# A chain of two attention and two Mamba layers on one core: softplus gathered in one visit, norm shifts moved from GpSimd to VectorE, C rows later in their queue, and a new order

## What is computed

```python
xz = einsum('bsd,ed->bse', xn, in_proj_w);  x_in, z = split(xz, 2)
u = silu(conv1d(x_in) + conv_b)                    # 512 channels, 4 taps
dt_r, B, C = split(einsum('bsd,ed->bse', u, x_proj_w), [64, 80])
dt = softplus(einsum('bsr,dr->bsd', dt_r, dt_proj_w) + dt_proj_b)
A = -exp(A_log)                                    # 16 states per channel
def step(h, inp):
    dt_t, B_t, C_t, u_t = inp
    h = h * exp(dt_t[:, :, None] * A) + (dt_t * u_t)[:, :, None] * B_t[:, None, :]
    return h, einsum('bdn,bn->bd', h, C_t)
y = (scan(step) + u * D_param) * silu(z)
out = x + gate * einsum('bsd,ed->bse', y, out_proj_w)
```

## Time and profile before

| | us |
|---|---|
| median of 3 runs | 2023.14 |
| lowest of 3 runs | 2008.57 |
| the profiled execution | 2021.5 |
| its span, first to last instruction | 2019.3 |

### The profile page before, as it was taken

One profiled execution on the slowest core, in us unless ns is written; L12 is line 12 of the kernel. 1 busy time (PEld: TensorE's weight loads), 2 busy tenths in 40 slices (PEclk: granted clock), 3 DMA queues, 4 the chain that ended last, 5 costly groups with the idle time before them and its releaser, 6 DMA issues. The chain is left out here.

```text
span 2019.3 us, 29111 instructions
## 1 busy us (share of the span) xinstructions
PE 1817.7 (90%) x9252; PEld 1265.7 (63%) x9252; DVE 1780.9 (88%) x1818; ACT 1710.2 (85%) x3224; POOL 1789.5 (89%) x823
## 2 busy tenths in 40 slices
PE   8979688998989999998999999898998999697778
PEld 7555555757667575766667575656757575455666
DVE  5458999889999999999989999999989999898983
ACT  2488788989989999999989999999989998777662
POOL 0059999999999999999999999999999999999970
PEclk8989699999999999999999999999999999898999
DMA  7034554444445545454444545445444545454430
GB/s 279 1 110 156 169 165 149 139 159 155 150 140 171 167 146 181 130 182 153 146 150 152 178 149 175 147 157 162 157 140 155 166 154 180 142 162 142 155 105 11
DMA packets 163784, 302.29 MB, mean 150 GB/s; under 512 B 18904, under 2 KB 27312, under 8 KB 162096
## 3 DMA queue, kind: packets, MB, share of 16 engines
q1 hardware_dynamic: 153110, 287.45, 43.9%
q10 hardware_dynamic: 10522, 12.99, 2.1%
HBM read 292.98 MB, written 5.29 MB: 148 GB/s over the span
## 5 line engine op out<-in xcount | busy, mean ns | idle before, releaser
L969 POOL TENSOR_TENSOR state<-state,c_rows 128x1024 f32<-128x1024 f32 x510 | 1197.2, 2382 | 26.3 <-DVE state L1578 13.6
L1581 DVE TENSOR_TENSOR_SCAN state<-decay,mix_banks 128x512 f32<-128x512 f32 x576 | 673.1, 1206 | 15.7 <-ACT decay L1303 0.7
L2016 PE MATMUL bank<-const_sb,state 128*128 128x128 f32 x4096 | 546.4, 281 | 38.1 <-POOL state L969 37.7
L2016 PEld LDWEIGHTS bank<-const_sb,state 128*128 128x128 f32 x4096 | 482.1, 145 | 145.9 <-issue 76.4
L1578 DVE TENSOR_TENSOR_SCAN state<-mix_banks,state 128x512 f32<-128x512 f32 x448 | 525.4, 1204 | 48.0 <-ACT mix_banks L1284 36.4
L960 POOL TENSOR_TENSOR state<-kept,b_rows 128x1024 f32<-128x1024 f32 x224 | 532.4, 2381 | 19.7 <-DMA b_rows<-flat_rows 10.3
L1303 ACT ACTIVATE decay<-kept,ssm_pack 128x512 f32<-128x512 f32 x576 | 395.2, 716 | 17.0 <-DVE state L1581 14.2
L1571 DVE TENSOR_TENSOR mix_banks<-kept,mix_banks 128x1024 f32<-128x1024 f32 x288 | 353.5, 1227 | 42.4 <-ACT mix_banks L1292 33.6
L1284 ACT ACTIVATE mix_banks<-kept,ssm_pack 128x512 f32<-128x512 f32 x448 | 302.0, 683 | 57.4 <-DVE state L1581 42.2
L1836 PE MATMUL bank<-kept,conv_diag 128*128 128x512 f32 x496 | 225.3, 597 | 4.3 <-ACT kept L1224 3.8
L987 ACT ACT_TABLE_LOAD x165 | 211.7, 1283 | 8.8 <-issue 5.8
(11 more groups left out here) (206 smaller groups left out, 2237.9 us busy)
## 6 DMA issues: line engine op xcount, KB each, us to landing
b_rows<-flat_rows SPq DMA_DIRECT2D x512, 256.0 KB, 3.9
c_rows<-flat_rows SPq DMA_DIRECT2D x512, 256.0 KB, 3.6
conv_diag<-conv_diag SPq DMA_DIRECT2D x8, 1024.0 KB, 7.3
out<-x_res ACTq DMA_DIRECT2D x8, 512.0 KB, 3.2
ssm_pack<-ssm_pack SPq DMA_DIRECT2D x2, 1907.0 KB, 12.4
x_next<-x ACTq DMA_DIRECT2D x6, 512.0 KB, 6.7
x_again<-x_dbl ACTq DMA_DIRECT2D x16, 128.0 KB, 4.3
state<-ada_w SPq DMA_DIRECT2D x1, 1536.0 KB, 14.3
```

What stands on the lines that cost most here:

```text
L969: pool.tensor_tensor(st, st, by_pair(c_rows[:, row % ROWS]), ALU.mult).then_inc(m_prod, 1)
L1581: ins = dve.tensor_tensor_scan(st, decay[:, nth(g) % DECAYS], mixed, 0.0, ALU.mult, ALU.add)
L2016: ins = pe.matmul(y_banks[c2][:, t * P:(t + 1) * P], state[:, g % STATES, t * P:(t + 1) * P], ident, start=False, stop=(g == BANK_SUMS[g / ...
```

## The change

Five things are done.

1. The step sizes of both halves are made at the end of `before`: `steps` and `soft` of the second half stand behind those of the first, and from the second block on ScalarE takes the four softplus in one visit to the softplus tables. The fills dt2 and dt3 move from `TAIL_FILLS` to the ends of `PREP_FILLS`.
2. As the second half of the scan ahead still reads its step sizes then, odd scans put theirs in a new tile, `dt_late` (4 KB a partition). `step_sizes` of the second half stays in `tail`, and reads the tile that `dt_half` gives.
3. `shift` moves from POOL to VectorE, between the moments and `normed`.
4. In `feed` the C rows come three places behind the B rows in place of one (`C_BEHIND`).
5. All tables of the order are new: `STEPS`, `ATT_STAGES`, `PREP_STAGES`, `POST_STAGES`, `TAIL_STAGES`, `GATES`, `SKIPS` and the bases. `KINDS` and the amounts of banks, decays, states and rows stay.

The core of the diff; of the tables only a few lines:

```diff
-FIRST_BASES = {'att': (-53, -28), 'setup': -49, 'prep': -33}
-TAIL_BASE, POST_BASE, PREP_BASE = -19, -50, 8
-ATT_BASES, LATE_BASES = (18, 100, 153, 222), (41, 193)
+FIRST_BASES = {'att': (-54, -29), 'setup': -49, 'prep': -33}
+TAIL_BASE, POST_BASE, PREP_BASE = -1, -33, 9
+ATT_BASES, LATE_BASES = (15, 100, 153, 219), (42, 193)
...
+C_BEHIND = 3
...
-              "dtr", "dt0", "soft0", "soft1", "mul", "skip0", "last")
+              "dtr", "dt0", "soft0", "dt2", "soft2", "mul", "skip0", "last")
...
-TAIL_NAMES = ("dt2", "soft2", "soft3", "mul", "skip1")
+TAIL_NAMES = ("mul", "skip1")
...
-PREP_FILLS = (("turn0", "x0", "x2", "v0", "z0", "z2", "v2", "xp", "dt0"),
-              ("turn1", "x1", "x3", "v1", "z1", "z3", "v3", "dt1"))
-TAIL_FILLS = (("dt2",), ("dt3",))
+PREP_FILLS = (("turn0", "x0", "x2", "v0", "z0", "z2", "v2", "xp", "dt0", "dt2"),
+              ("turn1", "x1", "x3", "v1", "z1", "z3", "v3", "dt1", "dt3"))
...
+        dt_late = sb("dt_late", [P, HC, T])
...
         def dt_fills(si, h):
-            return [(tail_fill if h else prep_fill)(si, f"dt{h * HC + k}") for k in range(HC)]
+            return [prep_fill(si, f"dt{h * HC + k}") for k in range(HC)]
+
+        def dt_half(si, h):
+
+            return dt_late[:] if h and si % 2 else dt[:, h * HC:(h + 1) * HC]
...
-                for g in range(HALVES * N + 1):
+                for g in range(HALVES * N + C_BEHIND):
...
-                    if g > 0:
-                        slot, n = (g - 1) % ROWS, (g - 1) % N
-                        past(sp, m_prod, si * HALVES * N + g - ROWS)
+                    if g >= C_BEHIND:
+                        g -= C_BEHIND
+                        slot, n = g % ROWS, g % N
+                        past(sp, m_prod, si * HALVES * N + g + 1 - ROWS)
...
-            def shift(norm, root, done, k):
-                pool.wait_ge(root, k)
-                pool.tensor_tensor(norm["shift"][:, :, 0], norm["minus"][:, :, 0], norm["rstd"][:, :, 0],
-                                   ALU.mult).then_inc(done, 1)
...
-                pool.tensor_tensor(dtu[:, c], dt[:, c], u[s][:, c], ALU.mult).then_inc(p_dtu, 1)
+                pool.tensor_tensor(dtu[:, c], dt_half(si, h), u[s][:, c], ALU.mult).then_inc(p_dtu, 1)
...
                 for k, place in enumerate(dt_fills(si, h)):
                     at = h * HC + k
-                    yield from w.to(f"soft{at}")
+                    if k == 0 and (h == 0 or si == 0):
+                        yield from w.to(f"soft{at}")
                     table(SOFTPLUS)
                     src, done = filled(act, place)
-                    read_until = max(0, (si - 1) * UNITS + (h + 1) * HALF_UNITS)
+                    read_until = max(0, (si - 1 - h) * UNITS + (h + 1) * HALF_UNITS)
...
-                    act.activation(dt[:, at, :], src[:], ACT.Softplus,
+                    act.activation(dt_half(si, h)[:, k, :], src[:], ACT.Softplus,
...
                     yield from gates_activated()
+                yield from soft(w, pi, layer, 1)
                 yield from scaled(w, pi, layer, s, 0)
...
             def tail(si, layer, s):
                 w = Walk(TAIL_STAGES[si])
-                yield from soft(w, si, layer, 1)
                 yield from scaled(w, si, layer, s, 1)
...
+            def shift(norm, root, done, k):
+                dve.wait_ge(root, k)
+                dve.tensor_tensor(norm["shift"][:, :, 0], norm["minus"][:, :, 0], norm["rstd"][:, :, 0],
+                                  ALU.mult).then_inc(done, 1)
...
+                yield from w.to("root")
+                shift(att_norm, a_root, a_rstd, 2 * ai + 1)
                 yield from w.to("xn")
...
+                yield from w.to("dt2")
+                steps(pi, layer, 1)
...
             def tail(si, layer, s):
-                w = Walk(TAIL_STAGES[si])
-                yield from w.to("dt2")
-                steps(si, layer, 1)
+                yield from ()
```

More of the change, by code:

```diff
@@ L235 @@
-    7: (61, 75, 77, 80, 92),
-    8: (74, 88, 89, 90, 94),
-    9: (63, 75, 77, 81, 89),
-    10: (62, 75, 77, 81, 90),
-    11: (62, 75, 76, 84, 91),
-    12: (69, 88, 90, 91, 94),
-    13: (62, 75, 76, 77, 89),
-    14: (56, 75, 80, 83, 89),
-    15: (59, 74, 77, 82, 87),
+    0: (33, 36),
+    1: (1, 3),
+    2: (10, 19),
+    3: (13, 18),
+    4: (8, 18),
+    5: (14, 18),
+    6: (16, 19),
+    7: (16, 19),
+    8: (17, 19),
+    9: (3, 14),
+    10: (4, 18),
+    11: (11, 17),
+    12: (8, 17),
@@ L249 @@
 STEPS = {
-    "bank": (5, 7, 1, 5, 2, 5, 9, 3, 8, 8, 8, 8, 9, 4, 9, 5, 3, 5, 10, 8, 10, 7, 8, 8, 7, 8, 10, 8, 8, 7, 8, 8, 11,
[14 rows of a table removed]
-    "row": (6, 2, 7, 8, 7, 5, 11, 8, 8, 6, 8, 12, 3, 4, 8, 10, 8, 8, 2, 7, 12, 8, 7, 3, 11, 7, 6, 8, 8, 11, 6, 8,
[8 rows of a table removed]
-    "beside": (11, 9, 19, 21, 24, 27, 36, 37, 2, 3, 13, 8, 10, 12, 32, 34, 18, 19, 30, 33, 44, 24, 27, 29, 34, 37,
[22 rows of a table removed]
-    "inject": (14, 28, 29, 27, 19, 18, 14, 3, 19, 27, 24, 17, 14, 11, 10, 10, 11, 12, 16, 19, 4, 10, 10, 12, 10,
[8 rows of a table removed]
-    "weight": (11, 7, 10, 5, 9, 8, 6, 8, 9, 14, 14, 11, 15, 13, 12, 8, 7, 8, 12, 7, 5, 8, 6, 12, 11, 19, 17, 14,
[18 rows of a table removed]
@@ new lines @@
+    "row": (7, 1, 7, 4, 7, 6, 9, 8, 8, 4, 6, 12, 3, 5, 2, 8, 7, 8, 2, 4, 11, 5, 5, 6, 12, 8, 7, 7, 8, 11, 4, 8, 4,
[8 rows of a table added]
+    "beside": (6, 8, 19, 22, 25, 27, 38, 13, 2, 5, 4, 7, 11, 12, 30, 33, 18, 19, 30, 33, 44, 39, 27, 29, 38, 6, 4,
[22 rows of a table added]
+    "inject": (13, 29, 29, 28, 29, 25, 18, 15, 17, 17, 16, 18, 24, 23, 9, 17, 30, 25, 22, 26, 8, 11, 15, 12, 10,
[8 rows of a table added]
+    "weight": (10, 5, 10, 6, 8, 8, 6, 11, 11, 10, 10, 9, 13, 9, 14, 12, 12, 11, 9, 13, 8, 14, 12, 12, 5, 13, 12,
[18 rows of a table added]
+    "sum": (31, 28, 25, 23, 20, 16, 13, 10, 16, 14, 12, 9, 12, 10, 18, 15, 19, 16, 28, 32, 28, 25, 22, 18, 17, 15,
[39 rows of a table added]
+}
@@ L406, with fill_at @@
 ATT_FILL = att_bank_counts()
-def fill_at(names, what, preps, tails, posts):
+def fill_at(names, what, preps, posts):
     bank = 0 if what in names[0] else 1
@@ L412, in fill_at @@
     in_first = len(FIRST_PREP_FILLS[bank]) - len(PREP_FILLS[bank]) if preps else 0
-    before = in_first + len(PREP_FILLS[bank]) * preps + len(TAIL_FILLS[bank]) * tails + len(POST_FILLS[bank]) * posts
+    before = in_first + len(PREP_FILLS[bank]) * preps + len(POST_FILLS[bank]) * posts
     return bank, before + names[bank].index(what)
@@ L915, in setup @@
                 yield from ()
-            def shift(norm, root, done, k):
-                pool.wait_ge(root, k)
-                pool.tensor_tensor(norm["shift"][:, :, 0], norm["minus"][:, :, 0], norm["rstd"][:, :, 0],
-                                   ALU.mult).then_inc(done, 1)
             def attention(ai, layer, s, b):
-                w = Walk(ATT_STAGES[ai])
-                yield from w.to("root")
-                shift(att_norm, a_root, a_rstd, 2 * ai + 1)
-                yield from w.to("yroot")
-                shift(att_norm, a_root, a_rstd, 2 * ai + 2)
+                yield from ()
             def step_sizes(si, s, h):
@@ L934, in step_sizes @@
                 past(pool, m_scan, si * UNITS - (HALVES - 1 - h) * HALF_UNITS)
-                pool.tensor_tensor(dtu[:, c], dt[:, c], u[s][:, c], ALU.mult).then_inc(p_dtu, 1)
+                pool.tensor_tensor(dtu[:, c], dt_half(si, h), u[s][:, c], ALU.mult).then_inc(p_dtu, 1)
             def before(pi, layer, s, b):
                 w = Walk(PREP_STAGES[pi])
-                yield from w.to("root")
-                shift(prep_norm, p_root, p_rstd, pi + 1)
                 yield from w.to("mul")
@@ L1505, in attention @@
                     moments(att_norm, y, vector_link, a_var)
+                yield from w.to("yroot")
+                shift(att_norm, a_root, a_rstd, 2 * ai + 2)
+                if (ai, 1) in VECTOR_NORMS:
                     yield from w.to("yn")
@@ L1522, in before @@
                     moments(prep_norm, src, link, p_var)
+                yield from w.to("root")
+                shift(prep_norm, p_root, p_rstd, pi + 1)
+                if pi in VECTOR_PREPS:
                     yield from w.to("xn")
```

96 lines of the change are left out of this document (45 added, 51 removed), and 428 rows, old and new, of tables (ATT_STAGES, PREP_STAGES, STEPS).

## The result

The changed kernel took 2064.87 us (median of 4 runs, 2056.87 to 2070.93) beside 2020.12 us of the kernel before in the same comparison: a ratio of 1.0239, with a 95% interval from 1.017 to 1.0307. The ratios leave out one slow execution of 3804.73 us of the kernel before (without it its median is 2017.09) and one of 2665.65 us in experiment 6, which the medians in us count. The changed kernel is slower by 2.4%. The forecast was 2002 us; the time lies where rival A put it, between its middle of 2047 and its upper end of 2072.

A forecast was written before the change was run, and what follows sets the result against it. POOL's product stream, 1848.8 us with 62.5 us idle, was taken as the bound. Terms -6.3 - 6 - 4 - 7 + 0 + 3 + 1 = -19.3 from 2021.5 gave 2002 us, range 1970 to 2035.

The forecast's parts named there:

- rival A: VectorE shifts reading two SBUF operands stand until POOL's current product ends, up to 2.38 us each; middle 2047 us, chance 0.15.
- Shifts arrive on VectorE: 42 stream shifts at 0.18 us plus 7.9 us of root waits on VectorE: +3 us, bounds 0 and +15.5.
- The share of 0.21: Part of a VectorE stall taken to reach POOL: POOL's 26.6 us of waits over VectorE's 126.4 us idle.
- Shifts leaving POOL: 42 tiny products leave POOL's stream, -6.3 us, and its waits there for the reciprocal root go, -6 us.
- C rows, -7: C rows later in the queue cut POOL's 10.3 us of B-row waits: -7 us, bounds +4 and -10.3.
- Step sizes, -4: POOL's 8.6 us idle before step-size products, mostly for softplus, shrinks: -4 us, bounds +5 and -8.6.
- Softplus in one visit: 32 fewer ScalarE table loads, 41 us, against a new wait for PE's bank refill: 0 us, bounds -26.6 and +27.
- The hole: ScalarE visit of at least 6.2 us delaying VectorE's decays and B-row copies: 27 us of VectorE, 5.7 us of POOL.
- The order anew: New order's effect on POOL's remaining waits for VectorE and PE: counted as nothing, between -10 and +20 us.
- The marks named ahead: For: stream near 1830 us, B-row waits within 3, 133 loads; against: late shifts or scans, POOL's VectorE waits above 40.

The follow-up runs named there:

- experiment 6: Changed kernel with each shift on VectorE as four 128x1 products of two tensors: 2127.22 us, ratio 1.0562.
- experiment 3: Changed kernel with each shift on VectorE as four 128x1 products taking the reciprocal root as per-partition scalar operand: 1997.84 us, ratio 0.9928.
- experiment 11: Changed kernel with scalar-operand shifts for the 16 Mamba norm shifts alone, the 32 of the attentions keeping two tensors: 2048.07 us, ratio 1.0188.
- experiment 8: Kernel before with scalar-operand shifts on VectorE and C rows three places behind the B rows: 2023.63 us, ratio 1.0049.
- experiment 5: Kernel before with shifts on VectorE as four 128x1 products with a per-partition scalar, old order and C rows: 2024.53 us, ratio 1.0057.
- experiment 7: Changed kernel with scalar-operand shifts and C rows one place behind the B rows again: 2067.52 us, ratio 1.0266.

## Why the prediction was wrong, step by step

**Where it failed: "Shifts arrive on VectorE".** I took 0.18 us a shift, from the earlier trace rows, which were measured while POOL stood still; in the stream it was 2.07. The term came out as +3 with an upper bound of +15.5, though rival A's own working gave up to 100 us of VectorE for the same 42 instructions. So the bound of the term did not hold the uncertainty that the text named, rival A had too small a chance (0.15) for something that no row spoke against, and the range ended at 2035, below A's middle. The scalar form takes the price away, and 63 us with it (experiment 3, control 6).

The price was not all that the step had wrong. With the measured price its own sum would have been (42 x 2.07 + 5.9) x 0.21 = 19.5 us in place of +3, and the forecast about 2019, still inside the range. The share of 0.21, POOL's waits for VectorE over VectorE's idle time, was no measure of a stall of this kind: each microsecond more in the shifts was about one more of the span (0.9 to 1.1 in the table behind experiment 11).

**Rival A's mechanism was right, and its price nearly.** It took at most one product, 2.38 us, for a shift. The mean was 2.07, but made of many shorter stalls and eight longer ones. By A's own sum VectorE then needs 1653.6 + 42 x 2.07 + 70 = 1810.5 us of its 1780: 2052. The profiled execution was 2060.76. That it comes so near is luck in part. The 70 are the waits for ScalarE of the kernel before; in the changed kernel the same two rows (shown below) have 22.0 + 21.6 = 43.6, and with these the sum gives 1784 and 2026. What else lengthens the stream is open; POOL's pauses behind the eight long stalls, 23.1 us, may be a part.

**The sum without the stall came close by luck.** Forecast were 2002 of 2021.5, a ratio of 0.990; experiment 3, the change without the stall, has 0.9928 (0.9912 to 0.9944). But two errors, of 25 and 20 us, cancel in it. Shifts and C rows together were to give -6.3 - 6 - 7 + 3 + 1 = -15.3 us, and in the old order they cost 10 (experiment 8, 1.0049). Step sizes, visit and order were to give -4 and gave -24 (experiment 3 against 8). Term by term:

- Shifts leaving POOL, -6.3 and -6: in the old order the move, arrival included, costs 11.8 us (experiment 5). VectorE gets 27.2 us of products and waits 11.9 for the root; POOL's waits for scans grow by some 16. That is a share of 16 / 39 = 0.4, where I had 0.21, an average over stalls of all kinds.
- C rows, -7: alone in the old order -7.7, with the row that the step named (10.3 to 3.2 us). In the new order the part is a condition, not an addition (experiment 7), and four waits for B rows are left, 8.6 us, all but 0.2 of it before 180 us.
- Step sizes, -4: POOL's idle time ahead of these products fell in the window from 6.9 us to 2.4 + 1.0, as the step said; what that is worth by itself was not tried.
- Softplus in one visit, 0: 133 loads and a wait for PE's refill, as forecast. The waits are 24.3 us in 16, 1.5 each, where I had 1.13:

```profile
ACT dt_late L1152 <- PE bank L1794: 12.5, 8, 2.2
ACT kept L1152 <- PE bank L1794: 11.8, 8, 2.2
```

The hole does not show in VectorE's waits as I feared. Its waits for decays and copies fell, from the 36.4 + 33.6 of the earlier trace rows:

```profile
DVE state L1582 <- ACT mix_banks L1275: 22.0, 25, 2.5
DVE mix_banks L1575 <- ACT mix_banks L1283: 21.6, 17, 4.1
```

- The order anew, 0: together with the visit worth 24 us (experiment 8 against 3), more than the -10 that I had allowed the order alone, but inside the bounds of the two together (-36.6).

**The marks named ahead.** Two of those that were to speak against the forecast came: the scan behind the shift starts late again and again (A), and POOL's waits for VectorE stand at 67 us, above 40. C rows as a wait of POOL did not come. Of the marks for the forecast, the 133 table loads came; the stream (1892.5 us, not near 1830), the shifts and the waits for B rows (8.6 us, not under 3) missed.

**The version that beats both** is experiment 3: 0.9928 of the kernel before, 14.8 us less, and 63 less than the changed kernel.

## What to carry to other kernels

Before an instruction is moved to VectorE beside a busy POOL, look at where its operands lie. Two tensors in SBUF can cost a whole POOL product or several, however small the instruction; a per-partition scalar as second operand did not, nor did a second tensor in PSUM. A duration taken from an opening, where the other engine stood still, is no price for the stream, and an average share of waits no measure of what a new stall will cost. In a kernel whose order is written out as a whole, parts do not add up: what is worth 8 us alone can be worth nearly 70 in the order that counts on it, so undo the suspect and keep the rest.

## What was not expected of the hardware

All 42 shifts in the stream lasted until a POOL product ended, 34 of them until the one in progress did. Eight stood through one to four further products that POOL began later, up to 9.71 us, and ended only when POOL paused. So one product, 2.38 us, which rival A took as its most, is no bound here. The Trainium skill (SBUF — State Buffer, Who interferes with whom) says that a VectorE instruction with two SBUF inputs and a GpSimd one that reads SBUF exclude each other, and that the second to start stands until the first ends. The trace agrees for the 34; for the eight it differs, since products that started after the shift still went ahead of it.
